# The cross attention of a decoder layer: fp32 on array tiles in place of split fp32r products, a pair of sequences at a time

## The reference

```python
x = x + lightning_attention(layernorm(x))       # 32 heads of 128, silu, decay, gate, rms norm
# per sequence b, with C = 64 channels and T = 512 positions (a sequence is read as 64 x 512)
q = einsum('dc,bct->btd', Wq, ctx) + bq;  k = einsum('dc,bct->bdt', Wk, ctx) + bk
attention = softmax(einsum('btd,bds->bts', q, k))          # 512 x 512
v = einsum('oc,bct->bto', Wv, layernorm(x)) + bv
x = x + einsum('bts,bsc->bct', attention, v)
x = x + einsum('bsd,ed->bse', layernorm(x), identity)
```

## Time and profile before

| | us |
|---|---|
| median of the runs | 2416.9 |
| profiled execution, time | 2418.2 |
| profiled execution, span | 2416.4 |
| TensorE matmul busy | 2355.1 (97%) |
| VectorE busy | 1280.6 (53%) |
| ScalarE busy | 792.8 (33%) |
| GpSimd busy | 631.8 (26%) |

### The profile page before, as it was taken

One profiled execution on the slowest core, in us unless ns is written; L12 is line 12 of the kernel. 1 busy time (PEld: TensorE's weight loads), 2 busy tenths in 40 slices (PEclk: granted clock), 3 DMA queues, 4 the chain that ended last, 5 costly groups with the idle time before them and its releaser, 6 DMA issues. The chain is left out here.

```text
span 2416.4 us, 38134 instructions
## 1 busy us (share of the span) xinstructions
PE 2355.1 (97%) x15104; PEld 1988.5 (82%) x15104; DVE 1280.6 (53%) x1769; ACT 792.8 (33%) x1384; POOL 631.8 (26%) x520
## 2 busy tenths in 40 slices
PE   8999999999999999999999999999999997999997
PEld 6888888888888888888888888888888886677775
DVE  5654535454545454444444444444454545988986
ACT  3232222222322222222222222222222323776774
POOL 2321111121212121212111111121212223666663
PEclk9999999999999999999999999999999998999999
DMA  3010101010000000000000000001010102101100
GB/s 133 1 45 1 45 0 44 0 35 9 27 17 27 17 27 17 27 17 27 17 27 17 27 18 18 26 1 43 0 44 0 42 1 101 35 30 35 39 30 18
DMA packets 26991, 65.88 MB, mean 27 GB/s; under 512 B 3536, under 2 KB 6352, under 8 KB 26832
## 3 DMA queue, kind: packets, MB, share of 16 engines
q1 hardware_dynamic: 26960, 65.43, 7.9%
HBM read 61.23 MB, written 4.19 MB: 27 GB/s over the span
## 5 line engine op out<-in xcount | busy, mean ns | idle before, releaser
L486 PE MATMUL bank<-xn_hi,w_hi 128*128 128x512 f32 x1536 | 613.8, 400 | 2.9 <-DVE w_lo L368 2.9
L488 PE MATMUL bank<-xn_hi,w_lo 128*128 128x512 f32 x1536 | 600.3, 391 | 0.0
L487 PE MATMUL bank<-xn_lo,w_hi 128*128 128x512 f32 x1536 | 599.6, 390 | 0.0
L250 POOL TENSOR_TENSOR sq<-attn 128x512 f32<-128x512 f32 x128 | 180.3, 1409 | 1543.6 <-ACT attn L322 1533.7
L486 PEld LDWEIGHTS bank<-xn_hi,w_hi 128*128 128x128 f32 x1536 | 288.9, 188 | 67.9 <-issue 3.2
L488 PEld LDWEIGHTS bank<-xn_hi,w_lo 128*128 128x128 f32 x1536 | 289.0, 188 | 61.7
L487 PEld LDWEIGHTS bank<-xn_lo,w_hi 128*128 128x128 f32 x1536 | 289.3, 188 | 56.5
L437 DVE TENSOR_TENSOR gate<-gate,attn 128x512 f32<-128x512 f32 x128 | 136.9, 1111 | 352.2 <-ACT attn L322 352.2
L531 PE MATMUL bank<-w_hi,xn_lo 128*128 128x256 f32 x1024 | 289.2, 282 | 0.0
L529 PE MATMUL bank<-w_hi,xn_hi 128*128 128x256 f32 x1024 | 289.2, 282 | 0.0
L530 PE MATMUL bank<-w_lo,xn_hi 128*128 128x256 f32 x1024 | 289.0, 282 | 0.0
(11 more groups left out here) (106 smaller groups left out, 3353.0 us busy)
## 6 DMA issues: line engine op xcount, KB each, us to landing
raw<-w_qkv SPq DMA_DIRECT2D x48, 512.0 KB, 3.6
raw<-w_gate SPq DMA_DIRECT2D x16, 512.0 KB, 4.0
raw<-w_out SPq DMA_DIRECT2D x16, 512.0 KB, 3.3
stage<-ctx_in SPq DMA_DIRECT2D x64, 128.0 KB, 2.6
xr<-x SPq DMA_DIRECT2D x4, 1024.0 KB, 9.8
out<-attn_acc SPq DMA_DIRECT2D x16, 256.0 KB, 2.0
attn_acc<-x SPq DMA_DIRECT2D x3, 1024.0 KB, 8.6
attn_acc<-x SPq DMA_DIRECT2D x4, 256.0 KB, 3.3
```

The source lines that it names most:

```text
L250: nc.gpsimd.tensor_tensor(sq[:, :], attn[:, h], attn[:, h], ALU.mult).then_inc(sq_made, 1)
L486: nc.tensor.matmul(dst, hi, xn_hi[:, c, s], start=(c == 0), stop=False)
L487: nc.tensor.matmul(dst, hi, xn_lo[:, c, s], start=False, stop=False)
L488: i = nc.tensor.matmul(dst, weights(w_lo, w, c, h), xn_hi[:, c, s], start=False, stop=(c == CH - 1))
```

## The change

The second half is rewritten; the first loses only the cuts at its end. One iteration now takes both sequences of a pair. Wq, Wk and Wv are laid out as block diagonals, so that one plain fp32 matmul over 128 rows projects both sequences of the tile. Scores are plain fp32 matmuls over 64 rows, sequence 0 on the upper and sequence 1 on the lower half of the array's rows, into two banks; one VectorE instruction takes the maxima of both. The product with the values is plain fp32 over 128 rows and 64 columns of the array, sequence 0 into the partitions 0 to 63 of bank 6 and sequence 1 into 64 to 127. Nothing is cut any more except the eye and xn3. The probabilities stay undivided and whole: a turned tile is copied out once (sequence 0 by ScalarE, sequence 1 by VectorE). The reciprocals are spread over the partitions by eight small matmuls with the identity (`spread_scale`), copied to SBUF, and the product is multiplied by them in `add_cross`, which also adds the bias of v (the weights of a row sum to one). Both banks of turned tiles (4 and 5) are used by each `turn`; q, k, scales, values, xn3 and the last layer share bank 7. The loops over pairs are written out. The context of a pair comes in one DMA.

```diff
--- before.py
+++ after.py
         self.ctx = stage[:, 0:2]
-        self.ctx_parts = sb("ctx_parts", [P, 2, D], F32R)
-        self.mats = sb("mats", [P, 4, P])
-        self.mats_hi = sb("mats_hi", [P, 4, P], F32R)
-        self.mats_lo = sb("mats_lo", [P, 3, P], F32R)
-        self.bqk = sb("bqk", [P, 2])
-        self.wv = sb("wv", [P, P])
+        self.wq = sb("wq2", [P, P])
...
+def load_ctx(sp, pre, t):
+    sp.dma_start(pre.ctx[:, t % 2], pre.ctx_in[t]).then_inc(pre.ctx_landed[t % 2], 16)
...
-        if tb == TB - 1:
-            act.wait_ge(pre.consts_landed, 16 * 7)
-            nc.scalar.activation(pre.mats_hi[:, :, :], pre.mats[:, :, :], ACT.Copy)\
-                .then_inc(pre.mats_hi_cut, 1)
-            for i in range(2):
-                cut_ctx_hi(nc, act, pre, i, 1)
...
-        if tb == TB - 1:
-            dve.wait_ge(pre.mats_hi_cut, 1)
-            nc.vector.tensor_tensor(pre.mats_lo[:, :, :], pre.mats[:, 0:3],
-                                    pre.mats_hi[:, 0:3].bitcast(F32), ALU.subtract)\
-                .then_inc(pre.mats_cut, 1)
...
-        q_parts = sb(own, "q_parts", [P, 2, D], F32R)
-        k_hi = sb(own, "k_hi", [P, 2, D], F32R)
-        k_lo = sb(own, "k_lo", [P, 2, D], F32R)
-        minus_max = sb(own, "minus_max", [P, 2, CH])
-        row_sum = sb(own, "row_sum", [P, 2, CH])
-        row_inv = sb(own, "row_inv", [P, 2, CH])
-        prob = sb(own, "prob", [P, 2, CH, D])
-        probT_hi = sb(own, "probT_hi", [P, 2, D], F32R)
-        probT_lo = sb(own, "probT_lo", [P, 2, D], F32R)
+        q = sb(own, "q", [P, 2, D])
+        k = sb(own, "k", [P, 2, D])
+        minus_max = sb(own, "minus_max", [P, 2, CH, 2])
+        row_sum = sb(own, "row_sum", [P, 2, CH, 2])
+        row_inv = sb(own, "row_inv", [P, 2, CH, 2])
+        prob = sb(own, "prob", [P, 2, 2, CH, D])
+        probT = sb(own, "probT", [P, CH, 2, D])
+        scale = sb(own, "scale", [P, D])
         xn2 = sb(own, "xn2", [P, D])
-        v_hi = sb(own, "v_hi", [P, CH, 2, P], F32R)
-        v_lo = sb(own, "v_lo", [P, CH, 2, P], F32R)
+        v = sb(own, "v2", [P, 2, CH, P])
...
+    for t in range(PAIRS):
+        if t + 2 < PAIRS:
+            sp.wait_ge(S["qk_mm"], 2 * t + 2)
+            load_ctx(sp, pre, t + 2)
+        if t >= 2:
+            sp.wait_ge(S["out_ready"], t - 1)
+            sp.dma_start(out_t[t - 2], x1[:, t - 2]).then_inc(S["stored"], 16)
+    for t in range(PAIRS - 2, PAIRS):
...
+    def exps(t, j, i, at):
+        act.wait_ge(S["max_ready"], t * CH + (j + 1))
+        nc.scalar.activation(prob[:, t % 2, i, j], bank[:, at + i], ACT.Exp,
+                             bias=minus_max[:, t % 2, j, i:i + 1],
+                             accum_out=row_sum[:, t % 2, j, i:i + 1]).then_inc(S["exp_ready"], 1)
+    def keep_turned(t, c):
+        act.wait_ge(S["turned"], t * CH + (c + 1))
+        nc.scalar.activation(probT[:, c, 0], bank[:, PT], ACT.Copy).then_inc(S["probT_a_ready"], 1)
...
+    keep_q(0, 6)
+    keep_k(0, 7)
+    for j in range(CH):
         for i in range(2):
+            exps(0, j, i, 2 * (j % 2))
+    keep_q(1, 4)
+    keep_k(1, 5)
     normed(2, 0, 0, xn2)
+    act.wait_ge(S["v_mm"], 1)
+    normed(2, 0, 1, xn2)
+    for c in range(CH):
+        act.wait_ge(S["eye_landed"], 16)
+        nc.scalar.activation(eye_hi[:, c], eye[:, c], ACT.Copy).then_inc(S["eye_hi_cut"], 1)
+    for t in range(PAIRS):
+        keep_turned(t, 0)
+        if t + 2 < PAIRS:
+            keep_q(t + 2, MISC)
+        keep_turned(t, 1)
+        if t + 2 < PAIRS:
+            keep_k(t + 2, MISC)
+        if t:
+            normed(3, 1, t - 1, xn3)
+        if t + 1 < PAIRS:
+            exps(t + 1, 0, 0, 0)
+        keep_scale(t)
+        if t + 1 < PAIRS:
+            exps(t + 1, 0, 1, 0)
+            exps(t + 1, 1, 0, 2)
+        keep_turned(t, 2)
+        if t + 1 < PAIRS:
+            exps(t + 1, 1, 1, 2)
+            exps(t + 1, 2, 0, 0)
+        keep_turned(t, 3)
+        if t + 1 < PAIRS:
+            exps(t + 1, 2, 1, 0)
+        if t:
+            xn3_high(t - 1)
+        if t + 1 < PAIRS:
+            exps(t + 1, 3, 0, 2)
+            exps(t + 1, 3, 1, 2)
+        if t + 2 < PAIRS:
+            act.wait_ge(S["v_mm"], t + 2)
+            normed(2, 0, t + 2, xn2)
...
+    def row_max(t, j, at):
+        dve.wait_ge(S["s_mm"], t * CH + (j + 1))
+        nc.vector.tensor_reduce(minus_max[:, t % 2, j], bank[:, at:at + 2], AX.X, ALU.max,
+                                negate=True).then_inc(S["max_ready"], 1)
+    def inverse(t):
+        dve.wait_ge(S["exp_ready"], 2 * CH * (t + 1))
...
+    def add_cross(t):
+        dve.wait_ge(S["pv_mm"], t + 1)
+        dve.wait_ge(S["scale_ready"], t + 1)
+        nc.vector.tensor_tensor(scale[:, :], bank[:, OUT], scale[:, :], ALU.mult)\
+            .then_inc(S["scaled"], 1)
+        dve.wait_ge(S["scaled"], t + 1)
+        nc.vector.scalar_tensor_tensor(out=x1[:, t], in0=scale[:, :], scalar=pre.bias[:, 2:3],
+                                       in1=x1[:, t], op0=ALU.add, op1=ALU.add)\
+            .then_inc(S["x2_ready"], 1)
+        dve.wait_ge(S["x2_ready"], t + 1)
...
     for j in range(CH):
+        row_max(0, j, 2 * (j % 2))
     dve.wait_ge(S["rrms_ready"], 1)
     dve.wait_ge(x_back[0], 16)
     make_x1(0)
     layernorm(2, 0, 0)
+    inverse(0)
     make_x1(1)
     dve.wait_ge(S["xn2_ready"], 1)
     layernorm(2, 0, 1)
+    keep_values(0)
+    for c in range(CH):
+        dve.wait_ge(S["eye_hi_cut"], c + 1)
+        nc.vector.tensor_tensor(eye_lo[:, c], eye[:, c], eye_hi[:, c].bitcast(F32),
+                                ALU.subtract).then_inc(S["eye_cut"], 1)
+    for t in range(PAIRS):
+        keep_turned(t, 0)
+        keep_turned(t, 1)
+        if t + 1 < PAIRS:
+            row_max(t + 1, 0, 0)
+            row_max(t + 1, 1, 2)
+        if t + 2 < PAIRS:
+            if (t + 2) % TT == 0:
+                dve.wait_ge(x_back[(t + 2) // TT], 16)
+            make_x1(t + 2)
+            dve.wait_ge(S["xn2_ready"], t + 2)
+            layernorm(2, 0, t + 2)
+        keep_turned(t, 2)
+        if t + 1 < PAIRS:
+            keep_values(t + 1)
+            row_max(t + 1, 2, 0)
+        keep_turned(t, 3)
+        if t + 1 < PAIRS:
+            row_max(t + 1, 3, 2)
+        if t:
+            xn3_low(t - 1)
+        if t:
+            dve.wait_ge(S["xn3_ready"], t)
+        add_cross(t)
+        layernorm(3, 1, t)
+        if t + 1 < PAIRS:
+            inverse(t + 1)
+        if t:
+            add_ffn(t - 1)
...
+    def project_q(t, at):
+        pe.wait_ge(pre.ctx_landed[t % 2], 16 * (t // 2 + 1))
+        nc.tensor.matmul(bank[:, at], pre.wq[:, :], pre.ctx[:, t % 2], start=True, stop=True)\
+            .then_inc(S["qk_mm"], 1)
+    def project_k(t, at):
+        nc.tensor.matmul(bank[:, at], pre.wk[:, :], pre.ctx[:, t % 2], start=True, stop=True)\
+            .then_inc(S["qk_mm"], 1)
+    def cross_scores(t, j, at):
         if j == 0:
+            pe.wait_ge(S["qk_ready"], 2 * t + 2)
+        for i in range(2):
+            s = slice(i * SEQ, (i + 1) * SEQ)
+            m = nc.tensor.matmul(bank[:, at + i], q[s, t % 2, j * P:(j + 1) * P], k[s, t % 2],
+                                 start=True, stop=True)
+        m.then_inc(S["s_mm"], 1)
+    def turn(t, c):
+        if c == 0:
+            pe.wait_ge(S["exp_ready"], 2 * CH * (t + 1))
+        if t or c:
+            pe.wait_ge(S["probT_a_ready"], t * CH + c)
+            pe.wait_ge(S["probT_b_ready"], t * CH + c)
+        for i in range(2):
+            for j in range(CH):
+                m = nc.tensor.transpose(bank[:, PT + i, j * P:(j + 1) * P],
+                                        prob[:, t % 2, i, j, c * P:(c + 1) * P], ident[:, :])
         m.then_inc(S["turned"], 1)
+    def weigh(t, c):
+        if c == 0:
+            pe.wait_ge(S["v_ready"], t + 1)
+            if t:
+                pe.wait_ge(S["scaled"], t)
+        pe.wait_ge(S["probT_a_ready"], t * CH + (c + 1))
+        pe.wait_ge(S["probT_b_ready"], t * CH + (c + 1))
+        for i in range(2):
+            s = slice(i * SEQ, (i + 1) * SEQ)
+            m = nc.tensor.matmul(bank[s, OUT], v[:, t % 2, c, s], probT[:, c, i], start=(c == 0),
+                                 stop=(c == CH - 1))
+        if c == CH - 1:
             m.then_inc(S["pv_mm"], 1)
+    def values(t):
         pe.wait_ge(S["xn2_ready"], t + 1)
         for c in range(CH):
+            s = slice(c * P, (c + 1) * P)
+            m = nc.tensor.matmul(bank[:, MISC, s], xn2[:, s], pre.wv[:, :], start=True, stop=True)
         m.then_inc(S["v_mm"], 1)
+    def spread_scale(t):
+        pe.wait_ge(S["inv_ready"], t + 1)
+        for j in range(CH):
+            for i in range(2):
+                m = nc.tensor.matmul(bank[i * SEQ:(i + 1) * SEQ, MISC, j * P:(j + 1) * P],
+                                     row_inv[:, t % 2, j, i:i + 1].broadcast_to([P, SEQ]),
+                                     ident[:, :], start=True, stop=True)
```

(100 more changed lines are left out.)

408 lines of the change are left out of this document (73 added, 335 removed).

## The result

The changed kernel takes 2359.8 us (median of four runs, 2359.1 to 2360.2) against 2416.9 for the kernel before: ratio 0.976, 95% interval 0.9747 to 0.9781. Predicted were 2385 us and a range of 2355 to 2430. The profiled execution has a span of 2357.7 us, 1.8 less than its time.

A forecast was written before the change was run, and what follows sets the result against it. VectorE and TensorE were taken to bound the kernel before together, TensorE's order alone the changed one. Start 2050.3 + pair 0 17.4 + 14 x 20.7 + last pair 27.2 = 2384.7 of span, forecast 2385 us, range 2355 to 2430.

The forecast's parts named there:

- rival A: The forecast itself, chance 0.58: tiles overlap in the second half, 2365 to 2405 us.
- pair 0's start by the walk's clock: Start of the second half: pair 0 begins at 2050.3 us of span, 9.5 later than before.
- the walk: One second-half pair on TensorE followed in program order, with waits for copies and maxima: 20.2 us a pair.
- pair 0: First pair of the second half, without a last layer, ending with the exponentials: 17.4 us.
- 14 pairs, each: Second-half loop: the walk's 20.2 us plus 0.5 for gaps, 20.7 us a pair against 22.6 before.
- last pair to the end: Last pair, without scores and projections, through a cold last layer, add and store: 27.2 us.
- Rival D: Chance 0.05: a fp32 record streams one cycle a column, a matmul takes 0.45 us; 2328 us.
- B: Rival, chance 0.18: streams of two row tiles don't overlap in the scores; 23.3 us a pair, 2425 us.
- n pairs cost n x 0.88 + 0.44: Groups of matmuls on two tiles: the second tile runs one record late; 2.2 us for scores 0 and 1.
- The 0.5 for gaps: Allowance in us a pair added to the walk, after 1.3 us a pair of uncounted gaps before.
- E: Rival, chance 0.09: waits the walk misses, or 1.2 GHz for part of each pair; 2400 to 2425 us.
- the walk's cold start: Start of the second half: q and k of pair 0 as cold fp32 matmuls, 4 x 0.85 us.

The follow-up runs named there:

- no_tiles: The changed kernel with scores, product with the values and spread scales all on the whole array instead of tiles: 2459.5 us, ratio 1.018.
- scores_by_tile: The changed kernel with scores 0 and 1 of a pair issued tile by tile instead of alternating: 2360.3 us, ratio 0.9765.
- before_light_low_parts: The kernel before, with the low part of the turned probabilities made for only 32 of 512 columns: 2402.2 us, ratio 0.9938.
- before_k_low_first: The kernel before, with VectorE making the low part of k ahead of the statistics of layer norm 3: 2433.9 us, ratio 1.0071.
- xn3_first: The changed kernel with xn3's low part ahead of the maximum of score 3 and its high part one exponential earlier: 2355.9 us, ratio 0.9748.
- divided_on_gpsimd: xn3_first with probabilities divided again, three quarters by GpSimd and the fourth by VectorE, without spread scales: 2368.1 us, ratio 0.9802.

## Why the prediction was right, and where its size was off

The sign and the mechanism held: tiles of both kinds run at once, and TensorE's list bounds the pair. The size did not: the time came out 25 us below the forecast and 5 below rival A's own range, inside the full one. By the steps of the sum:

| step | predicted | measured |
|---|---|---|
| pair 0's start by the walk's clock | 2050.3 | 2049.4 |
| pair 0 | 17.4 | 17.1 |
| 14 pairs, each | 20.7 | 18.91 |
| last pair to the end | 27.2 | 26.5 |

The start is the second turn's, 2051.27, less the walk's 1.87; pairs 1 and 15 start their first turns at 2066.48 and 2331.26, and (2331.26 - 2066.48) / 14 = 18.91. So 25 of the 27 us of span lie in one row.

- **fp32 pace**: right. 512 columns cost 0.43 us a record (eight in 3.43 in no_tiles), next to the upper bound of 0.44 that I took, an estimate from L1054's 0.11 for 128. Rival D, a fp32 record at the pace of fp32r (0.23), falls; the traces show steps in us and no cycles. That the load of 128 fp32 columns costs 0.11 shows in the trace of before: L512's load records start 0.11 us apart, as its matmul records of one column do.

```profile
2023.05 1.09 PEld L512 LDWEIGHTS bank<-ones,sq_acc 128*128 128x128 f32 x8
```

- **Tiles overlap**: right, on rows and on columns. On columns L546 had shown it for 64 columns: its records start two at a time, 0.007 us apart, 0.058 to the next two. For rows this was a choice that no row of before settled, the 58% against B's 18%. L570's loads and matmul records start two at a time as well, 0.112 to the next two, so its loads do overlap, but the 0.053 of its 64 columns (half of the 0.11 by which 128 lengthen a record, 0.17 to 0.276) is as much as its 0.056 a record. Two runs show what hung on it: either one going the other way is 45 us. The sign hung on it less than B said: with the row tiles gone the run still takes 2405.0 us, under the 2416.9 of before, because the rest of my sum was too long.

```profile
1010.83 1.86 PEld L570 LDWEIGHTS bank<-scores,v 64*128 64x128 f32 x32
```

- **The mis-sized term** is "n pairs cost n x 0.88 + 0.44" with 0.1 for the change of tiling. There is no late record: the second tile starts 0.007 us behind the first, and scores_by_tile shows that the order of issue doesn't bind the starts. A group of two pairs costs 1.92 or 1.81 us, where I had 2.2 and 0.1 more. Three of the four groups of a pair come out 0.4 to 0.5 shorter than in the walk (1.3 together), the fourth gives it up to the wait of 0.33, and the rest of the pair is 0.2 longer: 19.02 instead of 20.16, 1.1 us a pair.
- **The 0.5 for gaps** is the other half. I had found 1.3 us a pair in before that my count did not explain, and carried part of it over. The trace of before shows where they are: behind fp32 transposes, values or an idle time the first fp32r record of 512 columns takes a step of 0.31 to 0.34 us in place of 0.23. An ordinary pair of before has eleven such places, some 1.1 us.

```profile
2071.29 0.48 PE L1039 MATMUL bank<-probT_hi,v_hi 128*128 128x512 f32 x1
2071.61 0.40 PE L1040 MATMUL bank<-probT_lo,v_hi 128*128 128x512 f32 x1
2071.85 0.39 PE L1041 MATMUL bank<-probT_hi,v_lo 128*128 128x512 f32 x1
```

  After has a few of the kind (0.53 in place of 0.43 behind the first record of each projection); they are within the 0.2 above, so nothing was left for the 0.5. The 1.1 and the 0.5 are 1.6 us x 14 = 22 of the 25 us.
- **What bounds before**: half right. TensorE with VectorE's late results, yes. But before_light_low_parts shows that VectorE's load mattered little, and before_k_low_first that the order of its list mattered.
- **The clock**: the sum has nothing for it, and that was right: from 2052 to 2349 after has 1.00 granted. I missed that before paid for it in six pairs; 7.4 us of the gain are that. The lower level, of which E has a part, is 0.50 granted in the traces, and no run shows a frequency: before has it from 2027.5 to 2030.8, where the second half starts, and after from 2024.7 to 2035.0, where fp32 records of 512 columns start 0.85 us apart, as the walk's cold start had them. My sum went by lengths of after alone, so this did not hurt it.
- **VectorE, ScalarE**: 13.8 and 12.0 us a pair against 13.40 and 11.72; maxima over 1024 columns 1.22 as said. The 0.96 columns a ns in it is what VectorE's lengths give: 512 columns take 0.68 us and 32 take 0.18 (L881 in before_light_low_parts), 480 columns in 0.50; from 512 to 1024 it is 0.54. A copy out starts 0.31 us behind the start of the last transpose ahead of it in both kernels, which is the walk's 0.11 + 0.15 + 0.05. The walk's last layer would start without a wait of over 0.3; it waits for 0.33 on xn_lo, and xn3_first shows that the wait is worth 0.4 a pair and 4 us of the run.

## What to carry to other kernels

Two half-size fp32 matmuls on disjoint tiles of the array cost about one matmul's time here (1.92 or 1.81 us for eight records of 512 columns, against 3.53 on the whole array); without that, plain fp32 loses to three fp32r products here (2459.5 against 2416.9 us). Ahead of such a change, time one tile group with a long stream, since the rest of the sum hangs on it. A wait is not always removed by taking work off the engine or by moving one step. Moving xn_lo removed one; moving k_lo made the idle time longer, and the clock then fell in every ordinary pair. So look at what stood in the gap and what then comes behind. And don't carry an unexplained gap from the old loop into the estimate of a new one.

## What the runs showed of the hardware

- A change of tiling costs some 0.1 us each way. Behind the full-array projection the first score starts 0.52 us after the record ahead and the second pair of records 0.53 after the first, and what follows the last pair starts 0.52 after it, where the same steps are 0.43 in no_tiles. Eight score records take 1.92 us where 4 x 0.43 would be 1.72. The product takes 1.81 us behind the spread scales, which are column tiles too. In no_tiles scores, scales and product follow each other at their own pace (3.43 us for eight).
- The start of a matmul for an idle tile was not held by the one issued ahead of it for the other tile (1.92 us in either order), but its signal was: 2.01 us behind the group's start in scores_by_tile, 1.16 in the changed kernel.
- The first fp32r record of 512 columns behind fp32 transposes steps by 0.31 us or more in place of 0.23 (before, 2232 to 2254: 0.31 to 0.34).
- Of two VectorE multiplications of 128 x 512 in SBUF that start while GpSimd runs one of its own, the second takes 0.83 us in place of 0.48 (divided_on_gpsimd); it ends 0.28 us behind GpSimd's.
- The idle time of a pair does not settle by its sum whether the clock falls (to 0.50, for some 3.4 us a time). With 1.03 + 0.52 us it fell in 6 of 13 pairs, with 1.16 + 0.54 in 3 of 13, with 0.29 + 1.44 + 0.38 in all 13, and with 0.33 in none. The second periods of before and of before_k_low_first have 2.9 and 3.2 us of it and no fall. A fall cost 1.1 to 1.3 us in before and 1.5 to 1.6 in before_light_low_parts. What makes the difference stays open.
